# A state-space stage: ScalarE copies sums out of PSUM and GpSimd applies the gate

## The reference, cut to what matters

```python
xc = silu(conv(xt) + conv_b)                 # 512 inner channels
dBC = xc @ W_x.T                             # delta (64), Bm (16), Cm (16)
delta = softplus(delta @ W_dt.T + b_dt)
deltaA = exp(delta[..., None] * A)           # 16 states
BX = delta[..., None] * Bm[:, :, None, :] * xc[..., None]
hs = scan(h = deltaA * h + BX)               # along the 64 positions
y = einsum('bldn,bln->bld', hs, Cm) + Dp * xc
out = y * silu(z) @ W_out.T
```

## Time and profile before

| | us |
|---|---|
| median of 3 runs | 2384.08 |
| lowest, highest | 2381.45, 2387.69 |
| the profiled execution | 2398.74 |
| its span, first to last instruction | 2397.1 |
| TensorE busy in it | 1877.4 |
| VectorE busy | 1560.0 |
| GpSimd busy | 1244.9 |
| ScalarE busy | 1032.9 |

### The profile page before, as it was taken

One profiled execution on the slowest core, in us unless ns is written; L12 is line 12 of the kernel. 1 busy time (PEld: TensorE's weight loads), 2 busy tenths in 40 slices (PEclk: granted clock), 3 DMA queues, 4 the chain that ended last, 5 costly groups with the idle time before them and its releaser, 6 DMA issues. The chain is left out here.

```text
span 2397.1 us, 38628 instructions
## 1 busy us (share of the span) xinstructions
PE 1877.4 (78%) x11288; PEld 1301.8 (54%) x11289; DVE 1560.0 (65%) x3387; ACT 1032.9 (43%) x2950; POOL 1244.9 (52%) x1000
## 2 busy tenths in 40 slices
PE   5599977888897677999979999699547999988000
PEld 5378843333333243677647787587414888776000
DVE  5599938999999968333547777377696333333633
ACT  1376737665656314233247777333215333332000
POOL 1488616766767610688425555366002554543775
PEclk9799988999999977999989999899666999999555
DMA  6311013212212033899601110100503999998342
GB/s 204 106 74 70 11 33 142 78 65 67 75 43 99 0 118 101 197 299 257 149 14 32 32 37 19 29 2 2 189 0 109 285 281 280 276 252 204 111 116 83
DMA packets 163804, 272.04 MB, mean 113 GB/s; under 512 B 28722, under 2 KB 97300, under 8 KB 162708
## 3 DMA queue, kind: packets, MB, share of 16 engines
q1 hardware_dynamic: 130708, 199.72, 25.8%
q0 software_dynamic: 30464, 68.19, 12.4%
q10 hardware_dynamic: 2496, 2.44, 0.4%
HBM read 218.74 MB, written 51.53 MB: 113 GB/s over the span
## 5 line engine op out<-in xcount | busy, mean ns | idle before, releaser
L989 POOL TENSOR_TENSOR b_h<-b_h,b_bcb 128x1024 f32<-128x1024 f32 x128 | 301.9, 2359 | 151.5 <-DVE b_h L1046 150.8
L1558 POOL DMA_INDIRECT m1x_xb<-scratch_xn,m_tok x192 | 182.5, 951 | 336.2 <-DVE m1x_yb L1755 175.9
L814 PE MATMUL b_psy<-b_h,ident 128*128 128x512 f32 x512 | 252.9, 621 | 69.4 <-POOL b_h L989 69.2
L1046 DVE TENSOR_TENSOR_SCAN b_h<-b_dA,b_pbx 128x1024 f32<-128x1024 f32 x128 | 292.6, 2286 | 4.4
L1605 PE MATMUL m1x_psh<-m1x_xe,m1x_w 128*128 128x128 f32 x1536 | 211.4, 281 | 19.9 <-DMA m1x_w<-in_m_w 16.9
L1742 DVE TENSOR_TENSOR m1x_hT<-m1x_sg,m1x_psh 128x128 f32<-128x128 f32 x192 | 55.3, 288 | 235.5 <-ACT m1x_sg L1692 150.7
L814 PEld LDWEIGHTS b_psy<-b_h,ident 128*128 128x128 f32 x512 | 93.6, 193 | 210.4 <-POOL b_h L989 123.1
L945 ACT ACTIVATE b_dA<-b_delta,b_A 128x504 f32<-128x504 f32 x256 | 166.8, 706 | 93.2 <-DVE b_h L1046 87.7
L1605 PEld LDWEIGHTS m1x_psh<-m1x_xe,m1x_w 128*128 128x128 f32 x1536 | 190.4, 195 | 30.0 <-issue 18.1
L1928 POOL TENSOR_TENSOR x_s<-x_s,x_rs 128x1024 f32<-128x1024 f32 x64 | 121.2, 1893 | 126.9 <-DVE x_rs L2094 126.9
L1040 DVE TENSOR_TENSOR b_pbx<-b_pdx,b_bcb 128x1024 f32<-128x1024 f32 x128 | 157.6, 1231 | 19.8 <-ACT b_pdx L928 13.8
(11 more groups left out here) (452 smaller groups left out, 4424.9 us busy)
## 6 DMA issues: line engine op xcount, KB each, us to landing
m1x_w<-in_m_w SPq DMA_DIRECT2D x192, 256.0 KB
b_bcb<-scratch_bc_rows SPq DMA_DIRECT2D x64, 512.0 KB, 4.7
scratch_y<-m1x_yb SPq DMA_DIRECT2D x192, 128.0 KB
m_w<-in_m_w SPq DMA_DIRECT2D x64, 368.0 KB
a_c<-in_ctxT SPq DMA_DIRECT2D x16, 512.0 KB, 3.8
m_w<-in_m_w SPq DMA_DIRECT2D x64, 128.0 KB
x_area<-in_ctxT SPq DMA_DIRECT2D x32, 256.0 KB
m_w2all<-in_m_w SPq DMA_DIRECT2D x1, 8192.0 KB
```

The lines of the kernel that those rows point to most:

```text
L814: mm = pe.matmul(psy[:, k % 2, :], ident[:, :], h[:, u % HB, j, :], start=False, stop=(nq == NQ - 1 and j == CQ - 1))
L989: q.tensor_tensor(hs, hs, bcb[:, 1, CQ * nq:CQ * nq + CQ], ALU.mult).then_inc(sem("hc"), 1)
L1046: v.tensor_tensor_scan(h[:, u % HB].rearrange("p j n -> p (j n)"), dA[:, u % DB].rearrange("p j n -> p (j n)"), pbx[:, :, :].rearrange("p ...
L1558: g.indirect_dma_start(out=xb[:, j, :], out_offset=None, in_=xn, in_offset=bass.IndirectOffsetOnAxis(ap=tok[:, b:b + 1], axis=0)).then_inc ...
```

## The change

For 15 of the 16 chunks the gate product is split in two and leaves VectorE. ScalarE copies the chunk's sums from `psy` into `yz`, at unit 6 of the next chunk; the wait for the output projection of the group before goes with it. GpSimd then multiplies `yz` by `z` in place, ahead of unit 4 of the next chunk (ScalarE runs some steps ahead, so its unit 6 comes before GpSimd's unit 4). TensorE, before it begins a new chunk in a bank, waits for the copy and no longer for the gate product. The sixteenth gate product stays on VectorE as it was.

```diff
-        YZ, LAST = 2, 5
+        YOUT, YZ, LAST = 6, 4, 5
...
                     if nq == 0 and k >= 2:
-                        pe.wait_ge(sem("yz"), k - 1)
+                        pe.wait_ge(sem("y_out"), k - 1)
...
+                def sums_out(k):
+                    g, c = k // NCH, k % NCH
+                    a.wait_ge(sem("h_free"), NQ * (k + 1))
+                    if g and c == 0:
+                        s, n = bank("O", g - 1, 3)
+                        a.wait_ge(sem("psw_ready", s), n + 1)
+                    a.activation(yz[:, c, :], psy[:, k % 2, :], ACT.Copy).then_inc(sem("y_out"), 1)
+
                 for n, q, r in ahead(ACT_AT):
                     piece(n, q, r)
                 for g in range(NG):
                     for i in range(NU):
+                        if i % NQ == YOUT and NCH * g + i // NQ:
+                            sums_out(NCH * g + i // NQ - 1)
                         for n, q, r in due(ACT_AT, g, i):
                             piece(n, q, r)
                         decay(g, i)
...
+                def gated(k):
+                    g, c = k // NCH, k % NCH
+                    q.wait_ge(sem("y_out"), k + 1)
+                    q.wait_ge(sem("gate"), g + 1)
+                    q.tensor_tensor(yz[:, c, :], yz[:, c, :], z[:, c, :], ALU.mult).then_inc(sem("yz"), 1)
+
                 for n, w, c in ahead(POOL_AT):
                     piece(n, w, c)
                 for g in range(NG):
                     for i in range(NU):
+                        if i % NQ == YZ and NCH * g + i // NQ:
+                            gated(NCH * g + i // NQ - 1)
                         for n, w, c in due(POOL_AT, g, i):
                             piece(n, w, c)
                         weighted(g, i)
...
                 for g in range(NG):
                     for i in range(NU):
-                        if i % NQ == YZ and NCH * g + i // NQ:
-                            gated(NCH * g + i // NQ - 1)
                         for n, q, t in due(DVE_AT, g, i):
                             added(q, t)
                         scanned(g, i)
```

## The result

| | before | after |
|---|---|---|
| median, us | 2383.59 (4 runs, 2381.45 to 2387.69) | 2364.18 (4 runs, 2362.18 to 2366.68) |
| ratio, 95% interval | 1 | 0.9917 (0.9900 to 0.9935) |
| span of the profiled execution, us | 2397.1 | 2360.5 |
| first to last start of VectorE's product (L1040, after: L1058) | 482.1 | 464.7 |

The change takes 19.4 us off the time. The forecast was 17.7 us less, 2366.4 us. The two spans lie 36.6 us apart, and that must not be explained by the change. Between the starts of the stages (one `RECIPROCAL` each, L106) only one stretch besides the changed one differs by much (the others by at most 3.3 us): from the last of them to the end it is 2397.1 - 1690.9 = 706.2 us before and 2360.5 - 1666.7 = 693.8 after. That is the last mixture of experts, whose code is the same.

The account below looks back on a forecast made before the run. VectorE was taken as the bound, priced by the distance between starts of its product. 21.6 us leaving it less 3.9 given back through GpSimd's queue make 17.7 us off 2384.08: 2366.4 us, own bounds 2363 to 2370, range 2360 to 2377.

Parts of the forecast that it names:

- What leaves VectorE: Fifteen gate products and their waits leave VectorE's steps: 2.8 + 1.3 + 1.2 + 3.3 + 13.0 = 21.6 us.
- the three chunk-0 steps: Chunk 0 of groups 1 to 3: VectorE's gate product waits for the fourth output projection; 4.33 us each, 13.0 us saved.
- ScalarE's copies: Fifteen PSUM-to-SBUF copies of 0.59 us, 8.9 us in all, charged at nothing because ScalarE runs up to four steps ahead.
- The slack at step 24: Lead of ScalarE's decay over VectorE's scan behind the convolutions: 4.1 us before, forecast 2.8 us after, so no wait.
- Rival (b): ScalarE's slack at step 24 is gone and VectorE waits: 12 to 16.5 us given back, 2378 to 2383 us; chance 0.09.
- GpSimd's products: Step 4's product delays weightings, sums and the second projection, so VectorE's addition waits 1.3 us in three groups: 3.9 us back.
- rival (a): More GpSimd delay makes the fourth projection late; VectorE waits at its addition, leaving 8.6 us gain, 2375.5 us; chance 0.12.
- Others: TensorE's waits and SyncE's broadcasts cost nothing; ScalarE's fourth `z` copy waits perhaps 1 us, covered by its lead.
- The rule of the Trainium skill: Two-input elementwise work belongs on VectorE, GpSimd being about twice as slow; by it the stage would pay some 9 us.
- The sum: 21.6 less 3.9 = 17.7 us off the whole time: 2384.08 becomes 2366.4 us.
- (c): TensorE runs its full stretch (34 us without a gap) at its lower clock: 13 us slower, 2397 us; chance 0.05.
- (d): Projections keep their time and group 2's clock drop goes with the pauses: 21.6 us and a little more, 2361 us; chance 0.04.

Follow-up runs that it names:

- e1_dve_gate_later: Kernel before with its gate products still on VectorE, two steps later (ahead of a chunk's fifth step, not third): 2369.26 us, ratio 0.9933.
- the run with five pairs: Changed kernel with five further pairs of ScalarE activations (6.7 us) ahead of the decay of step 24 in every group: 2367.41 us.
- e2_gate_step2: Changed kernel, a group's last chunk copied ahead of ScalarE's step 5 and gated ahead of GpSimd's step 2 of the next group: 2360.29 us, ratio 0.9887.
- e4_pool_twice: Changed kernel with a second GpSimd pass (adding zero) over the same tile ahead of each of the 15 gate products: 2367.51 us, ratio 0.9916.
- e3_adds_later: Changed kernel with VectorE's additions of the output projection one step later (8, 9, 11, 12, not 7, 8, 10, 11): 2361.89 us, ratio 0.9892.
- e7_both_places: Changed kernel with GpSimd's group-boundary gate ahead of step 2 and VectorE's additions one step later: 2362.64 us, ratio 0.9901.
- before_again: Kernel before, unchanged, profiled once more: time 2389.82 us, span 2388.2 us, steps 482.1 us.
- the two runs with further activations: Changed kernel with two or five further pairs of ScalarE activations ahead of step 24's decay in every group: 2365.31 and 2367.41 us.

## Why the prediction was right

**What leaves VectorE** (21.6 us). Right in each part. Steps without a gate product are 3.58 to 3.59 us, in the first chunk 3.66, and the 13.0 us of the three chunk-0 steps are gone. That a gate product costs the 0.46 us between two starts and not its busy 0.66 is what made the sum right: at 0.66 for each of the 15 it would have been about 3 us too high. `e1_dve_gate_later` adds what the prediction did not say: most of that sum was never tied to the engine. It told correctly what the wait was for, but not that a later place on the same engine would pass it.

**ScalarE's copies** (nothing). Right. They take 578 ns in the median and VectorE waits for none of them. The wait for the fourth projection went to ScalarE, 6.7 us over three times, and is hidden there. The slack at step 24 was forecast as 2.8 us; it is 3.4 by the timeline and about 3 by the run with five pairs. Rival (b) was therefore near: five pairs of activations at that one place turn the 17.5 us gained in the steps into 6.

**GpSimd's products** (3.9 us given back). Right in mechanism, and in place for groups 1 and 3: the second projection, ahead of step 8. The cost there was worked out as 1.3 us and is 1.1, 0.95 of it ahead of step 8 and 0.15 ahead of step 7. In group 2 it is 1.8 us, and at the first projection, ahead of step 7, where the prediction had none; there TensorE was at its lower clock (below). That the sum came to 4.0 is in part luck: three groups at the full clock would have given 3.3 us, and the 0.7 us on top came from a fall of the clock that the prediction did not have in this place. The delay did not reach the additions of steps 10 and 11, so rival (a) did not come about, although its margin had been put at only 0.1 us.

**Others.** One size was missed. ScalarE's fourth `z` copy was put at "perhaps 1 us" of waiting for the gate product on GpSimd; it waits 7.0 us over three times, up to 2.4. The lead of ScalarE covered it, as said.

```profile
ACT b_z L922 <- POOL b_yz L1005: 7.0, 3, 2.4
ACT b_yz L955 <- PE b_psw L801: 6.7, 3, 2.2
```

**The rule of the Trainium skill** ("GPSIMD Engine Reference", "Engine selection") is confirmed in its ratio: 1266 ns for L1005 against 673 for the same product on VectorE, which read the sums from PSUM. Taken as a verdict on the change it would have misled, if by little: against the same products at the later place on VectorE (467.2 us) the move gained 2.6 us, with the place of `e2_gate_step2` 6.2 us, and fifteen further passes of GpSimd over the same tile cost the stage 2.7 us.

**The sum.** 482.1 less 21.6 plus 4.0 is 464.5; the steps are 464.7. The time moved by 19.4 us where 17.7 were forecast; the difference is within the spread of the runs, 4 to 6 us for either kernel. One thing stays open (each against the kernel before as it ran beside it, 2385.74 or 2384.52 us): `e2_gate_step2` came out 25.5 us below the kernel before in time and 21.1 in steps, and `e4_pool_twice` 18.2 and 14.8. The runs do not show where the other 3.4 and 4.4 us lie, or whether they are more than spread; in `e1_dve_gate_later` it is 1.6 us, in `e3_adds_later` 2.5, in `e7_both_places` 0.6. The profiled executions show how wide the spread is. Outside the changed stage (counted from its `RECIPROCAL` to the next stage's) the code is the same in all ten, and it took 1839.8 us in the kernel after, 1833.4 with five pairs, 1849.6 in `before_again` and 1859.3 in the first profile. A gain of a few us in this stage is therefore read from its steps, which repeat to 0.1 us for the kernel before, and to 0.7 us where the clock falls on other groups.

**Rivals (c) and (d).** TensorE's full stretch (after: 521.78 to 558.70 in group 1) ran at the full clock, 1.00, and so did the same stretch in group 2 (640 to 670). So (c) did not come about. Of (d), the pause of 3.67 us is gone but another took its place.

## What to carry to other kernels

Price an instruction on the bounding engine by the distance between two starts with and without it, and a wait apart from the instruction that carries it: here 14.9 of 21.6 us belonged to a place in the order, which one number moves. Before work goes to another engine's queue, read that queue step by step at the place where it is put in; over the stage GpSimd was idle for about a third of the time (336.6 of 487 us busy before), and in steps 3 to 5 it had no room at all. Then follow who stands behind it: GpSimd was not waited for by VectorE directly, but by way of TensorE's projections. The version to keep is the changed kernel with either of the two places moved, 460.8 to 461.0 us of steps in place of 464.7. By time (2360.3 and 2361.9 us against 2364.2, intervals overlapping) that is not told apart.

## What was not expected of the hardware

TensorE's clock fell behind shorter pauses than the 3.67 us of the kernel before, and not each time. In the kernel after it idled 2.15 us ahead of the sums of step 4 in group 1 and 2.13 us in group 2. Timeline of TensorE in both, and the stretches that follow:

```profile
502.47 1.98 PE L814 MATMUL b_psy<-b_h,ident 128*128 128x512 f32 x4 [2.15 <-POOL b_h L999]
...
619.81 3.37 PE L814 MATMUL b_psy<-b_h,ident 128*128 128x512 f32 x4 [2.13 <-POOL b_h L999]
```

```profile
502.00:507.00 5.00, 3.71 (x12) 2.20 (x12) 4.83 (x5) 4.95 (x6) 5.00 (x4) 1.00 0.00 0
...
619.00:624.00 5.00, 4.19 (x8) 2.19 (x9) 4.39 (x3) 4.95 (x6) 5.00 (x4) 0.66 0.01 3
```

In group 1 the granted clock stayed at 1.00, 2.4 GHz. In group 2 it was 0.66 on average, part of it at the lower level of 1.2 GHz, and the same four matmuls took 3.37 us, not 1.98. The same holds for the pause of 3.67 us before: no fall in group 1 (the sums behind it took 1.98 us), one in group 2. The price here was 0.7 us (9.39 against 8.69 us for steps 7 and 8). In the two runs with further activations, which have the same order in steps 0 to 8, it fell in groups 1 and 3, so that the step sums of equal orders can differ by 0.7 us for each.

The length of the pause alone did not decide. At the same place near the end of groups 1 and 2, the kernel after has the same pause of 1.73 us, behind 5.3 us in which TensorE was busy for 3.04 us both times. The granted clock of the next 5 us was 1.00 in group 1 and 0.66 in group 2:

```profile
590.80 1.99 PE L814 MATMUL b_psy<-b_h,ident 128*128 128x512 f32 x4 [1.73 <-POOL b_h L999]
```

```profile
708.85 3.65 PE L814 MATMUL b_psy<-b_h,ident 128*128 128x512 f32 x4 [1.73 <-POOL b_h L999]
```

What decides between the two stays open. VectorE lost nothing there: its steps are the same in both groups.
